# Attention and a quantized feed-forward on one core: the heads of four batches in one sequence of steps, and where the weights are put into groups of four

## What is computed

```python
# x: 4 batches x 512 tokens x 1024; ctx: 4 x 64 x 1024; H, KV, HD = 16, 4, 96
hidden = concatenate([ctx, layernorm(x)], axis=1)          # 576 rows per batch
q = (layernorm(x) @ Wq.T)                                  # 16 heads of 96
k, v = hidden @ Wk.T, hidden @ Wv.T                        # 4 groups of 96
attn = softmax(q @ k.T / sqrt(96)); out = attn @ v
x = x + out @ Wo.T
# feed-forward: layernorm, then three linear maps, 1024 -> 2752 (gate, up) -> 1024
# fake_quant: s = max(|t|) / 127 per row of t; q = round(t / s) * s
h = silu(fake_quant(ln) @ fake_quant(w_gate).T) * (fake_quant(ln) @ fake_quant(w_up).T)
x = x + fake_quant(h) @ fake_quant(w_down).T
```

## Time and profile before

| | before |
|---|---|
| median of three runs | 1632.27 us (1631.5 to 1632.86) |
| profiled execution | 1629.38 us |
| its span | 1627.3 us |
| granted PE clock, mean | 0.981 |
| PE busy | 1524.0 us, 94% |
| DVE busy | 1131.3 us, 70% |
| ACT busy | 634.6 us, 39% |
| POOL busy | 662.0 us, 41% |
| DMA, q1's share of 16 engines | 73.4% |
| first score tile | at 65.6 us |
| first matmul of the feed-forward | at 1156.7 us |

### The profile page before, as it was taken

How to read it: one execution, slowest core, us unless ns; L and a number is a source line. 1 busy time by engine, 2 the same in 40 slices (tenths; PEclk the granted TensorE clock), 3 DMA queues, 4 the chain that set the end, 5 groups by cost and what they waited for, 6 DMA issues and landing times.

```text
span 1627.3 us, 23751 instructions
## 1 busy us (share of the span) xinstructions
PE 1524.0 (94%) x8033; PEld 757.0 (47%) x8033; DVE 1131.3 (70%) x2020; ACT 634.6 (39%) x1162; POOL 662.0 (41%) x827
## 2 busy tenths in 40 slices
PE   6989989999987999989899989977999999999997
PEld 3544434654443465444346444433444444444443
DVE  5255674456678545677655677785599999999984
ACT  3366655146555415655541556653111111111110
POOL 3277787047768505767740577764000000000000
PEclk9999999999999999999999989998999999999999
DMA  7299999479999937979994999999963424234332
GB/s 244 73 259 218 227 254 236 135 210 219 214 233 228 221 119 218 237 189 215 234 209 152 267 233 246 209 260 205 306 173 82 106 66 103 82 82 106 82 93 57
DMA packets 482523, 297.30 MB, mean 183 GB/s; under 512 B 405709, under 2 KB 438273, under 8 KB 481281
## 3 DMA queue, kind: packets, MB, share of 16 engines
q1 hardware_dynamic: 482433, 296.15, 73.4%
HBM read 142.61 MB, written 46.69 MB: 116 GB/s over the span
## 4 chain that ended last, share of the span: by engine, by line
PE 57%; POOL 12%; DVE 11%; ACT 5%; issue 5%; DMA 5%; SPq 4%; DVEq 0%; ACTq 0%
PE ps_s L1483 17%; PE ps_g L1496 10%; PE ps_g L853 7%; PE ps_g L854 7%; PE ps_g L855 7%; POOL p_nat L831 5%; POOL p_f L826 4%; PE ps_s L948 3%; SPq L735 3%; DVE small L1156 2%; ACT p_nat L1056 2%; DVE small L1179 2%; DMA pT<-p_nat 2%; PE ps_o L963 2%; ACT p_f L1045 2%
## 5 line engine op out<-in xcount | busy, mean ns | idle before, releaser
L831 POOL TENSOR_TENSOR p_nat<-p_f,p_nat 128x512 f16<-128x512 f32 x256 | 311.8, 1218 | 159.4 <-ACT p_nat L1056 158.5
L826 POOL TENSOR_SCALAR p_f<-p_f,small 128x576 f32<-128x576 f32 x256 | 214.1, 838 | 294.0 <-DVE small L1161 293.1
L1056 ACT ACTIVATE p_nat<-p_f 128x576 f16<-128x576 f32 x256 | 174.4, 682 | 287.5 <-POOL p_f L826 279.8
L948 PE MATMUL ps_s<-k,q 96*128 96x512 f16 x768 | 225.3, 385 | 58.0 <-ACT p_f L1045 57.7
L1156 DVE TENSOR_REDUCE small<-ps_s 128x1 f32<-128x576 f32 x256 | 191.1, 747 | 59.5 <-PE ps_s L949 58.8
L1483 PE MATMUL ps_s<-w_gu_sb,xT 128*128 128x512 bf16 (+1 forms) x1152 | 226.2, 357 | 2.7 <-DVE g_sb L1582 2.7
L1045 ACT ACTIVATE p_f<-ps_s,small 128x576 f32<-128x576 f32 x256 | 186.9, 730 | 105.8 <-DVE small L1156 104.2
L1515 ACT ACTIVATE g_sb<-g_sb,sx 128x512 f32<-128x512 f32 (+1 forms) x128 | 74.5, 582 | 383.5 <-DVE g_sb L1582 331.8
L1461 POOL TENSOR_TENSOR rstd<-var_eps,minus_half 128x1 f32<-128x1 f32 x16 | 10.0, 628 | 427.4 <-DVE var_eps L1537 427.4
L1496 PE MATMUL ps_g<-w_dn_sb,hT 128*128 128x512 bf16 x704 | 161.0, 382 | 5.2 <-DMA hT<-h_int 5.2
L1483 PEld LDWEIGHTS ps_s<-w_gu_sb,xT 128*128 128x128 bf16 x1152 | 112.5, 98 | 113.8 <-DVE g_sb L1582 7.0
(11 more groups left out here) (114 smaller groups left out, 2555.3 us busy)
## 6 DMA issues: line engine op xcount, KB each, us to landing
w_in<-w_gu SPq DMA_DIRECT2D x40, 512.0 KB, 4.6
wq<-wq_c SPq DMA_DIRECT2D x36, 512.0 KB, 4.6
wo<-wo_c SPq DMA_DIRECT2D x24, 768.0 KB, 5.9
gu_q<-w_t SPq DMA_DIRECT2D x44, 256.0 KB, 3.2
w_in<-w_dn SPq DMA_DIRECT2D x8, 1376.0 KB, 7.0
x_acc<-x SPq DMA_DIRECT2D x4, 2048.0 KB, 8.4
x<-x_acc SPq DMA_DIRECT2D x8, 1024.0 KB, 5.1
x_ln<-x SPq DMA_DIRECT2D x16, 512.0 KB, 3.6
```

The lines of the kernel that those rows point to most:

```text
L826: nc.gpsimd.tensor_scalar(f, f, inv_sum[:, j % 2, t:t + 1], P_UP, ALU.mult, ALU.mult).then_inc(p_scaled, 1)
L831: nc.gpsimd.tensor_tensor(h[:, S + C:2 * S], f[:, 0:T], h[:, 0:T], ALU.subtract)
L948: nc.tensor.matmul(o[:, 0:T], l, k2[0:HD, hl, kv, 0:T], start=(i == 0), stop=(i == 2))
L1056: nc.scalar.activation(p_nat[:, t % NN, 0:S], p_f[:, tile(b, j, t) % NF, :], ACT.Copy).then_inc(p_high, 1)
```

## The change

The table of side work is by step number `s`, from 0 to 65, over all batches, with `b, j = divmod(s, H)`. The two drain steps are left only behind the last batch; elsewhere the last two heads' values fall into steps 0 and 1 of the next batch. Output units of groups 2 and 3 of a batch go into steps 0, 4 and 5 of the next one; keys for the next batch into steps 14 and 15; its values into its steps 1 and 2. Due times of high, low, rounding and residual are other ones, POOL's low half of a token tile is two instructions, `move_k` waits for the batch's last score tile as well, and `turn`, not `round_off`, reads every fourth column. The diff, cut to its core:

```diff
-HIGH, LOW = 3.7, 4.6
+HIGH, LOW = 5.0, 5.9
...
+def side_work(s):
+    b, j = divmod(s, H)
     q = [[("Q", kv, c) for c in range(QC)] for kv in range(KV)]
     o = [out_units(kv) for kv in range(KV)]
+    values = [("PV", *divmod(s - 2, H), t) for t in range(ST)] if 2 <= s < B * H + 2 else []
+    mine, before = [], []
+    if b == B:
+        ahead, mine, before = (([], [], SCALES + o[2][1:5]), ([], [], o[2][5:] + o[3]))[j]
+        return [], values, labelled(b - 1, before)
     if b == 0:
+        mine = {0: LATE_KEYS, 1: q[1][:1], 2: q[1][1:2], 3: q[1][2:], 4: q[2][:1], 5: q[2][1:2], 6: q[2][2:]}.get(j, [])
+    else:
+        before = {0: o[2][3:], 4: o[3][:5], 5: o[3][5:]}.get(j, [])
+        mine = {1: VALUES[:3], 2: VALUES[3:] + q[1][:1], 3: q[1][1:], 5: q[2][:1], 6: q[2][1:]}.get(j, [])
+    if b < B - 1:
+        mine = mine + {7: o[0][:5], 8: q[3][:2], 9: q[3][2:] + o[0][5:], 10: o[1][:3], 11: o[1][3:6],
+                       12: o[1][6:] + q[0][:1], 13: q[0][1:], 14: KEYS[:4], 15: KEYS[4:] + o[2][:3]}.get(j, [])
+    else:
+        if j == 6:
+            mine = q[2][1:2]
+        mine = mine + {7: q[2][2:] + o[0][:2], 8: o[0][2:5], 9: o[0][5:] + q[3][:1], 10: q[3][1:2] + o[1][:1],
+                       11: q[3][2:] + o[1][1:2], 12: o[1][2:5], 13: o[1][5:7], 14: o[1][7:], 15: o[2][:1]}.get(j, [])
+    side = labelled(b - 1, before) + labelled(b, mine)
+    n = len(side) // 3
+    if b and j == 1:
+        n = 0
+    elif b and j == 2:
+        n = len(side) - 1
+    return side[:n], values, side[n:]
...
+def step_order(s):
+    ahead, values, rest = side_work(s)
+    work = ahead + values + rest
...
+ORDER = [step_order(s) for s in range(B * H + 2)]
...
-LAND = 6.0
+LAND, KEPT, TURN = 6.0, 8.0, 6.0
...
-            t = max(t, (kept[-1] if both else kept[-2]) + LAND - 1.0)
+            t = max(t, (kept[-1] if both else kept[-2]) + KEPT)
...
-        pool += [(s + 2.5, "power", b, t), (s + 12.0, "tokens_lo", b, t)]
+        pool += [(s + 2.5, "power", b, t), (s + 12.0, "tokens_lo", b, t, 0), (s + 14.5, "tokens_lo", b, t, 1)]
...
-                if u == KEYS[-1]:
-                    sp.append((t + 8.0, "move_k", b))
-        sp.append((START[b] + 30.0, "residual", b))
+        sp.append((filled_at(b - 1, ("WO", KV - 1, TT - 1, 1)) + 8.0 if b else 30.0, "residual", b))
         if b < B - 1:
+            sp.append((max(filled_at(b, KEYS[-1]) + 8.0, END["S", b, H - 1, TT - 1] + 1.0), "move_k", b))
...
         def move_k(b):
             evacuated(sp, keys_use(0 if b is None else b + 1, QC - 1))
+            if b is not None:
+                sp.wait_ge(s_done, tile(b, H - 1, TT - 1) + 1)
...
+        def tokens_lo(b, t, h):
+            lo, x, hi = [a[:, o + h * 512:o + (h + 1) * 512] for a, o in
+                         ((halves(b, t), D), (token_tile(b, t), 0), (halves(b, t), 0))]
...
-            if j % G == 0 and kv >= 2:
-                filled(act, (b, ("WO", kv - 2, TT - 1, 1)))
+            if j % G == 0 and head(b, j) >= 2 * G:
+                filled(act, (b if kv >= 2 else b - 1, ("WO", (kv - 2) % KV, TT - 1, 1)))
...
             dve.wait_ge(w_up, lifts(g, h))
-            ins = nc.vector.tensor_scalar(to[:, :, 0:blocks, :],
-                                          w[:, 0:blocks * P].rearrange("p (k c m) -> p m k c", c=32, m=4), MAGIC, None,
-                                          ALU.subtract)
-            if rest:
-                ins = nc.vector.tensor_scalar(to[:, :, blocks, 0:rest],
-                                              w[:, blocks * P:].rearrange("p (c m) -> p m c", m=4), MAGIC, None,
-                                              ALU.subtract)
-            ins.then_inc(w_out, 1)
+            dve.wait_ge(w_turned, TURNS.index((g, h)))
+            nc.vector.tensor_scalar(w_int[0:rows, 0:cols.stop - cols.start], w_in[0:rows, n % 2, cols], MAGIC, None,
+                                    ALU.subtract).then_inc(w_out, 1)
...
-            nc.vector.transpose(w_t[0:rows, at:at + width], w_int[0:rows, 0:width]).then_inc(w_turned, 1)
+            nc.vector.transpose(w_t[0:rows, at:at + width].rearrange("p (m k c) -> p m k c", m=4, c=32),
+                                w_int[0:rows, 0:width].rearrange("p (k c m) -> p m k c", c=32, m=4)).then_inc(w_turned, 1)
```

More of the change, by code:

```diff
@@ L103, in cost @@
     if o[0] == "PV":
-        return (3 if o[2] < TT else 2) * 0.217
-    return COST[o[1][0]] / parts(o[1])
-def step_order(j, b):
-    side = [("X", u, i) for u in side_work(j, b) for i in range(parts(u))]
-    values = [("PV", j - 2, t) for t in range(ST)] if j >= 2 else []
-    n = len(side) // 3 if j < STEPS - 2 else 0
-    work = side[:n] + values + side[n:]
+        return (3 if o[3] < TT else 2) * 0.217
+    return COST[o[2][0]] / parts(o[2])
+def step_order(s):
+    ahead, values, rest = side_work(s)
+    work = ahead + values + rest
     total, done, order, k = sum(cost(o) for o in work), 0, [], 0
     for o in work + [None]:
-        while j < H and k < TT and (o is None or done >= total * k / TT):
-            order.append(("S", j, k))
+        while s < B * H and k < TT and (o is None or done >= total * k / TT):
+            order.append(("S", *divmod(s, H), k))
             k += 1
@@ L156, in pe_times @@
     starts, ends, t = {}, {}, 0.0
-    for b in range(B):
-        starts[b] = t
-        for o in batch_order(b):
-            c = S_COST if o[0] == "S" else cost(o)
-            starts[b, o], ends[b, o] = t, t + c
-            t += c
+    for s, step in enumerate(ORDER):
+        if s % H == 0 and s < B * H:
+            starts[s // H] = t
+        for o in step:
+            starts[o] = t
+            t += S_COST if o[0] == "S" else cost(o)
+            ends[o] = t
     starts[B] = t
@@ new lines, in engine_events @@
+    for o in (o for step in ORDER for o in step):
+        t = END[o]
+        if o[0] == "S":
+            b, j, k = o[1:]
+            dve.append((t + 0.1, "max", b, j, k))
+            dve.append((t + 2.0, "invert", b, j, k))
+            act += [(t + 1.0, "exp", b, j, k), (t + HIGH, "high", b, j, k)]
+            pool += [(t + 2.4, "scaled", b, j, k), (t + LOW, "low", b, j, k)]
+            sp.append((t + TURN, "turn_p", b, j, k))
+        elif o[0] == "PV" and o[3] == TT:
+            b, j = o[1:3]
+            act.append((t + 0.1, "out_hi", b, j))
+            dve.append((t + 0.9, "out_lo", b, j))
+            if HEADS[j % G] == G - 1:
+                sp.append((t + 2.5, "move_o", b, j // G))
+        elif o[0] == "X" and o[3] == parts(o[2]) - 1:
+            b, u = o[1:3]
+            if u[0] == "WO":
+                dve.append((t + 0.1, "add", b, u))
+            elif u[0] == "ST":
+                act.append((t + 0.1, "evac", b, u))
+                sp.append((t + 1.5, "scales_out"))
+            else:
+                act.append((t + 0.1, "evac", b, u))
+                dve.append((t + 1.6, "evac", b, u))
+            if u[0] == "Q" and u[2] == QC - 1:
+                sp.append((t + 3.2, "move_q", b, u[1]))
+            if u == ("WO", KV - 1, TT - 1, 0) or u == ("WO", KV - 1, TT - 1, 1):
+                sp.append((t + 1.0, "store_x", b, u[3]))
@@ L976, in tensor @@
                 unit[u[0]]((None, u), part, parts(u))
-        for b in range(B):
-            for kind, *a in batch_order(b):
+        for step in ORDER:
+            for kind, b, *a in step:
                 if kind == "S":
```

70 lines of the change are left out of this document (14 added, 56 removed).

## The result

The changed kernel takes 1625.4 us (median of 7 runs, 1618.1 to 1628.7) against 1632.9 us before (7 runs): ratio 0.9942, interval 0.9924 to 0.9961. So it is 6 to 12 us faster, where 54 were forecast; the time lies above the range. It moved the way that was forecast, by a sixth of the size.

The account below looks back on a forecast made before the run. Attention's 1091 us held 980 of matmuls and 111 of stalls and slow clock, laid to short steps where late helpers stop PE. Stalls after, 12 + 25 + 20 = 57, are 54 us less: 1578 us, range 1552 to 1612.

Parts of the forecast that it names:

- The mechanism: Attention: in short 11.2 us steps anything late becomes a PE wait; longer steps cover it, 54 us less stall.
- The end: Last five steps before the final drain, and that drain: 25 us of stalls stay, 15 to 31.
- the start: Heads 0 to 5 of batch 0: same work in the same order, 12 us of stalls stay, bounds 8 and 14.
- Slower: Third rival, hand-over of x in steps 5 to 7 of batches 1 to 3: 1640, 1662 us at worst; chance 0.05.
- the body's sum: Attention between start and end: stalls fall from 74 to 20 us, bounds 6 and 65.
- the tokens: Five steps where the next batch's tokens come in: 4 us lost, three times, 12 in all.
- the hand-over: Store of x and load of the residual, steps 5 to 7 of the next batch: 2 us, three times, 6.
- the rest: Remaining body steps, taken to be like the two from 333.0 that lost nothing: 2 us.
- signs of being wrong: 15 us steps losing over 1 us each, DMA share above 1.0 for whole batches, or DVE awaiting the residual in step 7.
- The bound from above: Hand-over of x: longest store landing plus residual and stuck issue less the cover, some 11 us a batch.
- Rounding: Contiguous copy on DVE: 35 us of DVE less, none on the path by itself; some 20 us of POOL returned.
- The first one: Helpers' throughput, the DMA share, bounds attention: halfway 1604 us, chance 0.23; the whole 1628 to 1632, chance 0.03.

Follow-up runs that it names:

- e8: e2 without the 36 reloads of query weights and PE's waits for them; 1586.7 us.
- e9: e2 without the 24 reloads of output weights and PE's waits for them; 1590.5 us.
- e12: e2 with the transposing DMA of each chances tile turning only 640 of 1152 columns; 1577.5 us.
- e1: The changed kernel with its query units spread, at most one in a step where the table allows it; 1632.9 us.
- e4: The kernel before with only the new rounding and turning; 1620.4 us, ratio 0.9922 to the kernel before.
- e3: The changed kernel with the old rounding and turning put back; 1630.8 us, ratio 0.9971 to the kernel before.
- e2: The changed kernel with the loads of the residual and of the first gate weights each in four pieces; 1607.5 us.
- e5: e2 with the 36 loads of query weights issued by ACT instead of SP; 1616.5 us.

## Why the prediction was wrong

**The mechanism was half right.** Long steps did cover the chain: the wait for the exponential fell from 58 to 13 us, and steps of 15 to 18 us mostly lose nothing (236.3 to 315.1: 79 us at a clock of 1.00). The end lost 22 (25 forecast), the start 15 (12), PE's work is 980, the feed-forward 471.5, the strided transposition 1.240 us (1.241 before). By the rule on lines of 16 bytes of the Trainium skill (SBUF — State Buffer, Door 1: The DMA port swizzle) the transposition was to stay as it is, and the trace agrees. Slower did not occur. The score tiles' 188 us is a slip, 256 times 0.73 is 187; the total of 1027 has it right. Two steps more are short than the text says, heads 6 and 8 of batch 3 (11.1 and 11.8 us); neither lost anything.

**The step that failed is the body's sum,** 4 + 4 + 4 for the tokens, 2 + 2 + 2 for the hand-over and "the rest lies in steps such as those from 333.0, which lost nothing: 2", 20 us with an upper bound of 65. It is 72: by its own terms, heads 9 to 13 of batches 0 to 2, where the tokens come in, lose 29 (12 forecast), steps 5 to 7 of batches 1 to 3, where x is handed over, 15 (6), and the rest 28 (2). The largest miss is the rest: long steps were to lose next to nothing, and twelve of the body's 43 lose 51 us, the largest of them with PE waiting for a transfer or for a copy behind one. Of the prediction's signs of being wrong this one came (1.2 us a long step on the average); the DMA share did not pass 1.0 for whole batches, and no add of DVE's waited for the residual. Three things were wrong behind it.
- The row for the rest was chosen by PE's work alone. The stretch from 333.0 has a DMA share of 0.76; the new body's windows have 0.89 to 0.95, but for one of 0.85 that lost nothing. The share was in the same row, and it had been read only for the rival. That transfers are what matters is shown by e8, e9 and e12, where they go and stalls go with them.
- A transfer moved is a transfer that collides elsewhere. The old drains have a DMA share of 0.67, 0.61 and 0.60, the first in rows 3, the second below. They were the transfers' slack as well as PE's, and the prediction counted them only as PE's. That backlogs were worked off there is argued, not measured; that pieces bring 18 us in the new order and 2 in the old one fits it.
- One transfer was not looked at: the query weights. The new table pairs query units, so a load of 5 us has to fit between one unit's end and the next but one's start; PE waits 17.8 us for it in seven places. e1 shows that this wait alone was not worth its size.

Head 15 of batch 1 and the two drain steps in the kernel before, columns as in rows 3:

```profile
540.10:611.20 71.10, 71.10 (x403) 39.51 (x404) 38.04 (x60) 18.61 (x33) 14.52 (x18) 1.00 0.61 162
```

**Hand-over of x.** Forecast 2 us a batch with 8 + 8.4 us against 18.2 of cover. The adds did not wait (1.0 us in all). What the load did was to hold up the transposes behind it: in batch 3 one landed after 11.4 us, and step 7 lost 7.1. In batch 1 the two behind it took 10.2 us to issue, but the 6.8 that step 6 lost there were for query weights issued before. The first gate weights, put aside because they "now go four steps earlier", stopped SP for 10 us by themselves and cost 8.5. The bound from above held; the path was another.

**Rounding.** 35 us of DVE were forecast and 22 came; "none of it is on the path" was wrong for the old order, where the rounding alone brings 13 us (e4), and near right for the new one (5 us, changed against e3). That the shorter copy gives POOL time back was forecast at 20 us and came as 22 (e4) and 24 (changed against e3). A lock between the two engines is what the Trainium skill names (SBUF — State Buffer, Who interferes with whom), and these numbers fit it. Whether PE's 13 us in e4 come from POOL's time or from DVE's shorter queue, no run separates.

**Rivals.** The first one is what happened, nearer to its whole (1628 to 1632) than to its half (1604); it had 0.26 in all. The mean share was in fact 0.90 before and after. Its argument, stretches at 1.0 lose, is borne out by e9 and e12; its form, a bound on the mean, is not quite: e2 takes 18 us off at the same bytes, so it is bursts of transfers that stop PE, on a mean that leaves little to work them off. How much of a burst's cost lies in SP's blocked queue and how much in the engines behind it stays open; e5 argues for the engines, with ACT's own order as its rival.

**Slow clock.** A long stop can cost twice, as at 431: the granted clock is 0.93 and 0.89 in the two lossy windows of batch 0, 1.00 in the one that lost nothing, and 0.96 over attention (0.97 before). PE's listed waits in attention add up to 75 us before and 70 now, the stalls to 111 and 109; a few long stops gave back in clock what was gained in waits.

## What to carry to other kernels

When a schedule is packed to fill one engine's idle time, read every other resource's share in the same rows, the DMA engines' above all: the idle stretch may be where their backlog was worked off. A row is a model for the packed stretch only if its shares of all engines match. When mending a traced stall moves it one step further three times, stop mending and take load away; a removal that nobody waited for (here 18 MB of reloads, 15 to 17 us) tells more than a wait removed.

## What had not been expected of the hardware

- The issue of a transposing DMA takes 1.4 us of SP's queue in the median and 10 us behind a transfer of 2.9 MB; with the large transfers split in four pieces of 0.5 to 0.8 MB, 3 and 6 us apart, the longest is 5.4. Plain loads issued by ACT took 0.33 us each in the same traffic.
- e2 beats both kernels: 1607.5 us, 18 below the changed one, with nothing left out.
